# Head attention of a graph network: value products in pairs of key groups, and a ring of ten head slots

## The reference, cut to what matters

```
h = jnp.maximum(_layernorm(x, axis=-1), 0.0)
Q = (h @ Wq + bq).reshape(Bs, Ns, NUM_HEADS, HEAD_DIM)      # K and V alike
scores = jnp.einsum('bnhd,bmhd->bhnm', Q, K) / scale
scores = scores + (1.0 - adj[:, None, :, :]) * -1000000000.0
attn = jax.nn.softmax(scores, axis=-1)
out = jnp.einsum('bhnm,bmhd->bnhd', attn, V).reshape(Bs, Ns, OUT_DIM)
x = x + out @ Wo + bo
```

## Time and profile before

| what | value |
|---|---|
| time, three executions | 12304.7 us median (12304.4 to 12308.56) |
| the profiled execution, its own time | 12303.05 us |
| its span in the trace | 12301.3 us |
| granted clock of TensorE, mean | 0.995 |
| PE busy | 11965.8 us (97%) |
| DVE busy | 10281.1 us (84%) |
| ACT busy | 9346.4 us (76%) |

### The profile page before, as it was taken

The page is one execution under the profiler, slowest core; times in us unless marked ns, Lnnn a source line. Parts: engine busy times, 40 slices in busy tenths (PEclk is TensorE's granted clock), DMA queues, the critical chain, the costliest instruction groups (busy, mean ns, idle before and its releaser), DMA issues.

```text
span 12301.3 us, 239883 instructions
## 1 busy us (share of the span) xinstructions
PE 11965.8 (97%) x106113; PEld 5936.3 (48%) x106113; DVE 10281.1 (84%) x12373; ACT 9346.4 (76%) x7633; POOL 458.4 (4%) x636
## 2 busy tenths in 40 slices
PE   7999999999999999999999999999999999999999
PEld 3333853338433384333843348433484334843348
DVE  4999849998599975999759997599975999759997
ACT  3898739987499874988748887489874898749986
POOL 1000000000000000000000000000000000000000
PEclk9999999999999999999999999999999999999999
DMA  2000320003200031000310003100031000310003
GB/s 74 19 21 22 105 80 22 18 22 113 76 18 18 24 117 69 18 18 26 125 59 18 18 27 132 52 18 18 31 137 43 18 22 29 140 38 19 21 32 106
DMA packets 206087, 609.72 MB, mean 50 GB/s; under 512 B 45440, under 2 KB 137216, under 8 KB 139520
## 3 DMA queue, kind: packets, MB, share of 16 engines
q1 hardware_dynamic: 184176, 450.72, 10.5%
q0 software_dynamic: 20880, 143.66, 3.1%
HBM read 556.47 MB, written 8.39 MB: 46 GB/s over the span
## 4 chain that ended last, share of the span: by engine, by line
DVE 52%; PE 45%; issue 1%; ACT 0%; SPq 0%; DMA 0%; POOL 0%; DVEq 0%
DVE E L881 34%; PE ps L1339 10%; DVE E L889 9%; PE ps L1443 8%; PE ps L1359 7%; PE ps L1456 4%; PE ps L1516 4%; PE ps L1423 4%; PE ps L1372 4%; DVE T L904 2%; PE ps L1502 2%; DVE E L879 1%; DVE HW L915 1%; DVE adj_ring L896 1%; PE ps L1322 1%
## 5 line engine op out<-in xcount | busy, mean ns | idle before, releaser
L611 ACT ACTIVATE E<-QB,KBP 128x2048 f32<-128x2048 f32 x3328 | 6398.1, 1994 | 740.0 <-PE ps L1359 722.3
L1359 PE MATMUL ps<-E,s_win 128*32 128x512 f32 x61440 | 6739.6, 594 | 104.0 <-DVE E L889 60.5
L881 DVE TENSOR_SCALAR E<-QA,KLO,KHI 128x2048 f32<-128x2048 f32 x4096 | 5252.8, 1339 | 20.0 <-DVE nmin L904 17.8
L1359 PEld LDWEIGHTS ps<-E,s_win 128*32 128x32 f32 x61440 | 1975.5, 110 | 4667.3 <-issue 4182.8
L1013 DVE CUSTOM_DVE_ANT_0 T<-ps,adj_ring 128x2048 f32<-128x2048 f32 x512 | 1171.6, 2288 | 88.9 <-PE ps L1423 86.2
L889 DVE SCALAR_TENSOR_TENSOR E<-QB,KBN,E 128x2048 f32<-128x2048 f32 x512 | 1200.3, 2344 | 0.0
L643 ACT ACTIVATE T<-T,nmin 128x2048 f32<-128x2048 f32 x512 | 1028.8, 2009 | 215.5 <-DVE nmin L1013 215.4
L1443 PE MATMUL ps<-ident,T 128*128 128x128 f32 x8192 | 1098.7, 277 | 15.7 <-DVE HT L975 12.3
L1443 PEld LDWEIGHTS ps<-ident,T 128*128 128x128 f32 x8192 | 913.5, 141 | 198.9 <-ACT PT L523 71.1
L523 ACT ACTIVATE AGG<-ps 128x512 f32<-128x512 f32 x224 | 126.7, 596 | 1012.5 <-PE ps L1339 980.9
L1339 PE MATMUL ps<-adj_res,H 128*128 128x512 f32 x2048 | 889.5, 592 | 0.0
(11 more groups left out here) (147 smaller groups left out, 7706.3 us busy)
## 6 DMA issues: line engine op xcount, KB each, us to landing
adj_ring<-in_adj SPq DMA_DIRECT2D x384, 1024.0 KB, 5.0
adj_res<-in_adj POOLq DMA_DIRECT2D x128, 1024.0 KB, 6.4
qcur<-AGG SPq DMA_DIRECT2D x896, 16.0 KB, 2.7
qcur<-HT SPq DMA_DIRECT2D x896, 16.0 KB, 2.2
HW<-in_x POOLq DMA_DIRECT2D x9, 1024.0 KB, 6.5
X<-in_x SPq DMA_DIRECT2D x128, 64.0 KB, 1.9
out_x<-X SPq DMA_DIRECT2D x8, 1024.0 KB, 16.9
wq_r<-in_L_gnn_Wq SPq DMA_DIRECT2D x4, 64.0 KB, 2.3
```

The costliest lines, as they stand in the source:

```text
L611: last = nc.scalar.activation(E[:, e_slot(t, k) + g, :], QB[:, :], ACT.Relu, bias=KBP[:, col:col + 1])
L881: last = nc.vector.tensor_scalar(dst, QA[:, :], KLO[:, col:col + 1], KHI[:, col:col + 1], ALU.max, ALU.min)
L1359: last = mm(ps[QROWS * g:QROWS * (g + 1), 4 * u + c, :], win, E[:, s + g, c * CH:(c + 1) * CH], start=(k == 0), stop=(k == NS - 1), tile_p ...
```

## The change

Two things are changed together.

1. `PT2` is gone. `T2` becomes a ring of ten head slots, each 2048 wide; step `s` uses slot `s % 10`. The transposed probabilities of a group are copied back into the 512 columns of the same slot that have just been transposed. With ten slots, the slot that `min2(s)` overwrites is free by the order of PE's program: the scores that it waits for stand behind the last value products that read the slot.
2. `values2` is called for two groups in a row, in every second step (groups `q - 2` and `q - 1` where `q` is even, that is, in the odd steps `s`), not for one group in each step. In the other steps (even `s`) `scores2(s)` takes the place of the value products: it stands between the transposes of head 2 and those of head 3. In the odd steps it stays at the end.

```diff
+T2_SLOTS = 10
+def t2_slot(t, h):
+    return (t * HEADS + h) % T2_SLOTS
...
-            T2 = sb("T2", [P, 2, HEADS, N], where=ph)
-            PT2 = sb("PT2", [P, 2, HEADS, CH], where=ph)
+            T2 = sb("T2", [P, T2_SLOTS, N], where=ph)
...
-                    evac(PT2[:, q % 2, h, :], ps[:, bank_of(("probs", q, h)), :]).then_inc(bank_act, 1)
+                    evac(T2[:, t2_slot(q // NC, h), (q % NC) * CH:(q % NC + 1) * CH], ps[:, bank_of(("probs", q, h)), :]).then_inc(bank_act, 1)
...
                 if 0 <= q < GROUPS:
                     for h in range(HEADS - 1):
                         probs_t2(b, q, h)
-                if 0 <= q - 1 < GROUPS:
+                pair = q % 2 == 0 and 2 <= q <= GROUPS
+                if pair:
+                    values2(b, q - 2)
                     values2(b, q - 1)
+                elif s < STEPS:
+                    scores2(b, s)
                 if 0 <= q < GROUPS:
                     probs_t2(b, q, HEADS - 1)
                 if s % HEADS == 2 and 0 <= s // HEADS - 2 < NT:
                     spread2(b, s // HEADS - 2)
                 if s % HEADS == 3 and 0 <= s // HEADS - 2 < NT:
                     output2(b, s // HEADS - 2)
-                if s < STEPS:
+                if pair and s < STEPS:
                     scores2(b, s)
```

More of the change, by code:

```diff
@@ L641, in exp2 @@
                 act.wait_ge(t2_rdy, s + 1)
-                T = T2[:, t % 2, h, :]
+                T = T2[:, t2_slot(t, h), :]
                 nc.scalar.activation(T, T, ACT.Exp, bias=nmin2[:, h:h + 1], scale=-1.0,
@@ L1013, in min2 @@
                 nc.vector.tensor_tensor_reduce(
-                    out=T2[:, t % 2, h, :], in0=ps[:, 4:8, :].rearrange("p c n -> p (c n)"), in1=ring[:, t % 2, :],
+                    out=T2[:, t2_slot(t, h), :], in0=ps[:, 4:8, :].rearrange("p c n -> p (c n)"), in1=ring[:, t % 2, :],
                     scale=1.0, scalar=BIG, op0=ALU.add, op1=ALU.min, accum_out=nmin2[:, h:h + 1]
@@ L1019, in evac2 @@
                 dve.wait_ge(pt2_ps, (b * GROUPS + q + 1) * HEADS)
-                nc.vector.tensor_copy(PT2[:, q % 2, HEADS - 1, :], ps[:, bank_of(("probs", q, HEADS - 1)), :]
+                nc.vector.tensor_copy(T2[:, t2_slot(q // NC, HEADS - 1), (q % NC) * CH:(q % NC + 1) * CH], ps[:, bank_of(("probs", q, HEADS - 1)), :]
                                       ).then_inc(bank_dve, 1)
@@ L1443, in probs_t2 @@
                     last = nc.tensor.transpose(ps[:, bank_of(("probs", q, h)), k * P:(k + 1) * P],
-                                               T2[:, t % 2, h, j * P:(j + 1) * P], ident[:, :])
+                                               T2[:, t2_slot(t, h), j * P:(j + 1) * P], ident[:, :])
                 last.then_inc(pt2_ps, 1)
@@ L1456, in values2 @@
                         last = mm(ps[HD * h:HD * (h + 1), 3, 0:P],
-                                  V[:, g * TPC + k, h * HD:(h + 1) * HD], PT2[:, q % 2, h, k * P:(k + 1) * P],
+                                  V[:, g * TPC + k, h * HD:(h + 1) * HD], T2[:, t2_slot(t, h), q % NC * CH + k * P:q % NC * CH + (k + 1) * P],
                                   start=(g == 0 and k == 0), stop=(g == NC - 1 and k == TPC - 1),
```

## The result

| | before | changed |
|---|---|---|
| time, median of four executions each | 12305.3 us (12304.4 to 12308.6) | 12612.2 us (12609.2 to 12613.6) |
| span of the profiled execution | 12301.3 us | 12607.4 us |
| attention window, PE busy | 98% | 86% |

The ratio is 1.025, with a 95% interval of 1.0237 to 1.0262: slower by 307 us. The forecast was 12592, in a range of 12535 to 12640.

What follows compares the result with a forecast made beforehand. PE's order was taken to set the pace, with a 3.59 us PE-DVE-PE loop just under its 3.84 us step. Tiles growing from 15.76 to 18.28 us, with graph ends, add 289 to 12303: 12592 us, range 12535 to 12640.

Steps and rivals of the forecast that it cites:

- the loop of 3.59 us: PE, DVE, PE from scores through the minimum to the next scores, on one set of banks: 1.23 + 2.22 + 0.14 us.
- a slack of 0.25 us: Kernel before: PE's step of 3.84 us leaves this much over the 3.59 us from scores to scores through DVE.
- The saving of 0.29 us for a merged pair: Value products of two groups together save one pair of tiling mode changes per two steps: 0.13 + 0.10 + 0.06 us.
- The ring costs nothing: Copies into the ten slots keep their size and engines, and the slots need no new wait: no cost by itself.
- The wait of 1.35 us in each even step: PE could start even-step scores after 2.24 us, but scores, minimum and next scores take 3.59 us, so PE waits.
- From even to odd step, 5.22 and 5.88 us: Time from even-step scores to odd-step scores in a tile's two pairs, set by PE's work plus bank waits.
- The wait for the bank after `spread2`: The next group's second-head transposes need head 3's bank, which DVE must first copy out: PE loses 0.39 us.
- The mask is covered: DVE at remainder 3: mask, copy and `add2` end at 6.9 us, before `min2` could start at 7.1: 0.2 us to spare.
- The sum: A tile goes from 15.76 to 18.28 us; 36 us a graph in all, 289 us over 8 graphs, giving 12592 us.
- The tail: End of each graph, after the last scores: three merged pairs and a partly covered last wait give about 1 us back.
- The clock: Rival: PE's stops also lower its granted clock in attention, about 250 us more, 12840 us; chance 0.06.
- the faster rival: Even-step scores start without a wait, so only the 66 us saved on mode changes and some tails show: about 12230 us; chance 0.03.

Runs made afterwards that it cites:

- the ring alone: The kernel before with the ten-slot ring and copies in place, PE's step order unchanged: 12303.1 us against 12303.7 on the same chip, ratio 1.0000.

## Why the prediction was right

- **What bounds before, and the loop of 3.59 us.** Right where it matters. The loop shows in the changed kernel as 3.55 and 3.66 us, and halving the minimum moves the change's cost from 307 to 47 us. Not right is that a slack of 0.25 us stood in every step and that scores hardly ever waited. The count of 25 adds up waits of PE's matmuls and of its weight loads, and it misses short waits, as idle time is counted from the modelled end of the last matmul. Into remainder 0 the kernel before can be at the bound already: the step from 1351.71 to 1355.70 is 3.99 us and not 3.84. Of the 0.15, some 0.05 stand at the scores, which start 0.23 us behind the read of the minimum, just as all scores of remainder 0 do in the changed kernel; 0.1 stands at the twelve transposes, which hold PE for 1.51 us (1352.72 to 1354.23) and not 1.41:

```profile
1352.72 1.58 PE L1443 MATMUL ps<-ident,T 128*128 128x128 f32 x12
```

```profile
1355.47 0.09 DVE L1013 DVE_READ_ACCUMULATOR2_ANT nmin<- 128x1 f32 x1
```

In the trace of before the scores stand 0.23 us behind the read in 56 of the 112 steps into remainder 0 from the eighth step of a graph on. With the halved minimum nearly all of these steps are 3.84 us. The forecast did not suffer, because its 15.76 us a tile was measured with these waits in it.

- **The saving of 0.29 us for a merged pair.** Right for the pair without extras: 0.27 where no wait is in the way. For the pair with `spread2` and `output2` it was too large: 0.13. In the change the odd steps hold the saving and the waits in the even steps outweigh it.
- **The ring costs nothing.** Shown by the ring alone.
- **The wait of 1.35 us in each even step.** Right: the scores of an even step start 3.55 and 3.66 us after those before instead of the 2.24 that PE's own work needs, so they wait 1.31 and 1.42 us. The rows show 1.08 and 1.17 us of idle time, which the profile counts from the modelled end of the last transpose, some 0.25 us after PE could have issued. 293.8 us in sum were foreseen as 280 to 310.
- **From even to odd step, 5.22 and 5.88 us.** Measured 5.27 and 5.95. The wait for the bank after `spread2` is there: transposes that could have followed at 1365.13 (1364.69 + 0.44) start at 1365.53, 0.40 later (0.39 predicted). The 0.05 to 0.07 more are scores that had been waiting and hold PE 1.03 us and not 1.01 (1363.12 to 1364.15), and sixteen transposes of 1.96 where 1.85 and a wait of 0.06 were put.
- **The mask is covered.** Right, by 0.1 us: DVE goes without a recorded idle time from the mask at 1367.93 to the minimum at 1370.29, 1.22 after the scores.
- **The sum.** A tile is 18.43 us where 18.28 was worked out. In 14 tiles and 8 graphs that is 17 us of the 20 by which 12592 was short. The term that was sized too low is the loop into remainder 0, 3.66 and not 3.59, along with the two gaps above; the price of a second wait could have been read from the trace of before (1355.47 to 1355.70, above) and was not. The tail gave back 1.1 us a graph (the last scores to the first transposes of the last layer, 3006.50 to 3025.49 before and 3082.84 to 3100.76 after), 1 predicted.
- **The rivals.** The clock stayed at 0.99 in the attention and 0.995 overall, as before. The saving on which the faster rival rests is real and needed the shorter minimum to show.

No version tried beats the kernel before and still does all of the work. The ring alone takes as long; the nearest of those with pairs spaces the scores and is 35 us slower.

## What to carry to other kernels

An engine that is 98% busy with no idle time may still be 0.25 us away from another bound. Before an order is changed on it, find each loop that runs through another engine and back (here: one set of banks, filled, read, filled again), take its length from places where the engines do wait, and keep at least that much work between its two ends in every step and not just on average. A short wait need not show as idle time: in the kernel before, the one at remainder 0 shows only when the start of the scores is set beside the read of the minimum that they wait for. Grouping like work to save changes of mode takes evenness away from exactly these loops, so the grouped block has to be balanced by other work on the other side.

## What the runs showed of the hardware

- The first scores of a tile, behind two waits, start 0.23 us after the read of the minimum; behind one wait they start 0.14 us after it. About half of the 0.09 us comes back, as the scores behind one wait then hold PE for 1.05 us and not 1.01.
- A group of value products on four column tiles holds PE for 1.01 us ahead of scores as ahead of transposes. Even so a step with the value products directly ahead of the scores is 0.08 to 0.24 us longer, 64 us over the run; 0.08 of it would be the early start that scores have behind transposes.
- Transposes that are copied back over the columns they were read from, on two engines, took no longer in the kernel with the ring alone (copies of 685 ns and transposes of 277 ns in both), with three engines working in the same buffer.
